# Attention's score maxima: 192 of 1024 pieces copied to SBUF by ScalarE and joined three at a time by VectorE

## The reference

```python
h = _layernorm(x) * (1 + ca) + sa
qkv = einsum('bsi,oi->bso', h, w_qkv) + b_qkv          # 16 heads of 16
attn = einsum('bhqd,bhkd->bhqk', q, k) * scale
attn = softmax(attn, axis=-1)                          # over 1024 keys
vals = einsum('bhqk,bhkd->bhqd', attn, v)
x = x + ga * (vals @ w_o.T + b_o)
# then: layernorm, a gate over 32 experts (top 6), experts, a shared expert
```

## Time and profile before

| What | Value |
|---|---|
| three runs | 1542.15, 1539.56, 1530.76 us (median 1539.56) |
| span of the profiled execution | 1412.3 us |
| TensorE busy | 1342.8 us (95%) |
| VectorE busy | 1134.9 us (80%) |
| ScalarE busy | 753.7 us (53%) |
| GpSimd busy | 606.9 us (43%) |

### The profile page before, as it was taken

The page is one execution under the profiler, slowest core; times in us unless marked ns, Lnnn a source line. Parts: engine busy times, 40 slices in busy tenths (PEclk is TensorE's granted clock), DMA queues, the critical chain, the costliest instruction groups (busy, mean ns, idle before and its releaser), DMA issues.

```text
span 1412.3 us, 30839 instructions
## 1 busy us (share of the span) xinstructions
PE 1342.8 (95%) x8191; PEld 672.8 (48%) x8192; DVE 1134.9 (80%) x2823; ACT 753.7 (53%) x1155; POOL 606.9 (43%) x782
## 2 busy tenths in 40 slices
PE   7997999999999999999999999999999999999895
PEld 4552222332333323323333232568788888888551
DVE  7886999999999999999999994566566656656588
ACT  3762477676767676777677768113343433334100
POOL 4000113143644534636346357527755555655300
PEclk9997799999999999999999999999999999999999
DMA  6898355533546345444464355947766665666698
GB/s 218 260 270 216 93 171 133 121 85 83 125 126 156 91 121 149 132 96 107 125 170 117 105 155 176 274 136 234 231 199 206 202 183 177 180 179 178 238 344 337
DMA packets 216958, 243.55 MB, mean 172 GB/s; under 512 B 93948, under 2 KB 181500, under 8 KB 216736
## 3 DMA queue, kind: packets, MB, share of 16 engines
q1 hardware_dynamic: 189328, 166.42, 43.6%
q0 software_dynamic: 21776, 68.07, 13.4%
q10 hardware_dynamic: 5760, 7.87, 1.7%
HBM read 133.98 MB, written 108.28 MB: 172 GB/s over the span
## 4 chain that ended last, share of the span: by engine, by line
PE 71%; DVE 13%; DMA 4%; issue 1%; SPq 1%; ACT 1%; POOL 0%; DVEq 0%; POOLq 0%
PE psO L1174 14%; PE ex_psGU L1682 13%; PE psE L1161 13%; PE psM L1151 9%; DVE piece_max L1048 9%; PE ex_psY L1697 7%; PE ex_psX L1671 3%; PE psM L505 2%; PE ex_psA L1691 2%; PE psGU L1495 1%; DMA wide<-results 1%; PE co_psS L1951 1%; PE late_psGU L1931 1%; PE late_psX L1942 1%; PE psM L524 1%
## 5 line engine op out<-in xcount | busy, mean ns | idle before, releaser
L1048 DVE TENSOR_REDUCE piece_max<-psM 128x1 f32<-128x512 f32 x1024 | 641.9, 680 | 27.3 <-PE psM L1151 24.0
L1115 ACT ACTIVATE wide<-psE 128x1024 f32<-128x1024 f32 x512 | 496.8, 1021 | 206.2 <-PE psE L1161 204.1
L1151 PE MATMUL psM<-wide 48*128 48x512 bf16 x1024 | 324.0, 395 | 19.9 <-DVE piece_max L1048 11.7
L1161 PE MATMUL psE<-wide 49*128 49x512 bf16 (+1 forms) x2048 | 328.7, 380 | 3.2 <-DMA wide<-maxima 2.8
L1763 POOL DMA_INDIRECT results<-vals_inv,places x223 | 213.9, 959 | 150.5 <-DVE vals_inv L1749 86.4
L1174 PE MATMUL psO<-wide 128*32 128x512 f32 x2048 | 273.6, 606 | 0.6 <-ACT wide L1115 0.6
L1151 PEld LDWEIGHTS psM<-wide 48*128 48x128 bf16 x1024 | 78.1, 93 | 348.1 <-DVE piece_max L1048 277.3
L1682 PE MATMUL ex_psGU<-wide,ex_xT 128*128 x892 | 231.3, 382 | 0.8 <-ACT ex_xT L1714 0.7
L1161 PEld LDWEIGHTS psE<-wide 49*128 49x128 bf16 (+1 forms) x2048 | 117.6, 95 | 92.3 <-issue 8.7
L1682 PEld LDWEIGHTS ex_psGU<-wide,ex_xT 128*128 128x128 f32 x892 | 152.1, 190 | 14.6 <-issue 2.3
L1714 ACT ACTIVATE ex_xT<-ex_psX 128x256 f32<-128x256 f32 x223 | 85.3, 383 | 121.3 <-PE ex_psX L1671 118.5
(11 more groups left out here) (281 smaller groups left out, 1262.8 us busy)
## 6 DMA issues: line engine op xcount, KB each, us to landing
wide<-qk_parts SPq DMA_DIRECT2D x384, 64.0 KB
wide<-results SPq DMA_DIRECT2D x16, 1536.0 KB, 9.5
rows<-lists SPq DMA_DIRECT2D x112, 160.0 KB
h2Ts<-lists SPq DMA_DIRECT2D x111, 160.0 KB
qk_parts<-parts SPq DMA_DIRECT2D x32, 384.0 KB, 3.1
xin<-in_x_dram SPq DMA_DIRECT2D x16, 512.0 KB, 4.2
v_values<-vst SPq DMA_DIRECT2D x32, 256.0 KB, 3.5
wide<-v_values SPq DMA_DIRECT2D x16, 512.0 KB
```

The lines of the kernel that those rows point to most:

```text
L1048: v.tensor_reduce(piece_max[:, qh, (x * PAIRS + h) * KT // QH + qt, kh:kh + 1], bank_of("piece", PIECES * group + n), AX.X, ALU.max, negat ...
L1115: nc.scalar.activation(probs[:, step % 2, 2 * pair:2 * pair + 2], psE[:, pair], ACT.Exp, scale=HD ** -0.5).then_inc(exp_ok, 1)
L1151: nc.tensor.matmul(bank_of(*user), qa[g][rows, h, qt * P:(qt + 1) * P], ka[g][rows, h, kh * 512:(kh + 1) * 512], start=True, stop=True).th ...
L1161: mm = nc.tensor.matmul(psE[:, pair, x], k[g][part, pair, kt * P:(kt + 1) * P], q[g][part, pair, qh * 512:(qh + 1) * 512], start=(q is qa) ...
```

## The change

ScalarE copies the third of the four pieces of a step to SBUF as bf16 in six of the eight steps of a half (p = 0, 1, 2 and 4, 5, 6), behind its exponentials, its hosted work and the copy of `psO`. These 192 pieces are not reduced by VectorE one by one. Three copies, lying side by side in one of two buffers (taken from `act_s` and from the last part of `x2`, which are not in use in attention), make a triple. VectorE joins a triple with three pairwise maxima that halve the width (512 to 256, 128, 64 for each of the three) and one negated reduction of 3x64. The first triple is joined in the step with p = 4, the second in that with p = 7: level 0 behind the first piece, levels 1 and 2 behind the second, the reduction behind the third. `finish` waits for the join too. The banks of the copied pieces are free once ScalarE's copy is done (`piece_held`), those of the others by `piece_read`, whose counts are adapted.

```diff
--- before.py
+++ after.py
@@ -734,6 +734,9 @@
     HALF_PIECES = PIECES // QH
     COLS = HG * KT // QH
     PAIRS = HG // 2
+    STEPS_HALF = HALF_PIECES // 4
+    HELD_PIECE, HELD_STEPS, TRIPLE = 2, (0, 1, 2, 4, 5, 6), 3
+    JOINED_IN = {4: 0, 7: 1}
     NGR = B * NG
     ALL = STEPS * NGR
     with ExitStack() as ctx:
@@ -747,14 +750,17 @@
         inverse = sb("inverse", [HG * HD, S // HD], F32)
         spare_to = env.h2Ts[:, 0].rearrange("p k t -> p (k t)").bitcast(I32).rearrange("p (e f) -> p e f", e=E)
         piece_max = sb("piece_max", [P, QH, COLS, 2], F32)
+        held = [of.bitcast(BF16)[:, 0:TRIPLE * 512].rearrange("p (n k) -> p n k", n=TRIPLE)
+                for of in (env.act_s[:].rearrange("p m t -> p (m t)"),
+                           env.x2[:, TPC * LAST:].rearrange("p i d -> p (i d)"))]
         neg_max = sb("neg_max", [P, HG * KT], BF16)
         neg_max_t = sb("neg_max_t", [P, HG * KT], BF16)
         psE = ctx.enter_context(nc.psum_tensor("psE", [P, 2, 2, 512], F32))
         psM = ctx.enter_context(nc.psum_tensor("psM", [P, RING, 512], F32))
         psO = ctx.enter_context(nc.psum_tensor("psO", [P, 512], F32))
-        (scored, exp_ok, summed, piece_done, piece_read, max_ready, max_stored, max_there, o_read,
+        (scored, exp_ok, summed, piece_done, piece_read, piece_held, joined, max_ready, max_stored, max_there, o_read,
          o_stored, den_stored, den_in, divided, inv_stored, ch) = (
-            env.sem("att_" + n) for n in ("scored", "exp_ok", "summed", "piece_done", "piece_read",
+            env.sem("att_" + n) for n in ("scored", "exp_ok", "summed", "piece_done", "piece_read", "piece_held", "joined",
                                           "max_ready", "max_stored", "max_there", "o_read", "o_stored", "den_stored", "den_in", "divided", "inv_stored", "chain"))
         env.inv_stored = inv_stored
         env.exp_ok, env.summed, env.piece_read, env.o_read, env.o_stored = exp_ok, summed, piece_read, o_read, o_stored
@@ -779,11 +785,26 @@
             c, w = divmod(step, WINDOW)
             return c - 1, w
 
+        def held_at(n):
+
+            return n % 4 == HELD_PIECE and n // 4 % STEPS_HALF in HELD_STEPS
+
+        def held_before(n):
+
+            halves, n = divmod(n, HALF_PIECES)
+            return len(HELD_STEPS) * halves + sum(held_at(m) for m in range(n))
+
+        def read_before(n):
+
+            return n - held_before(n)
+
         ring = Ring(HALF_PIECES, PIECES * NGR)
 
         def bank_of(*user):
 
             return psM[:, ring.bank[user]] if user in ring.bank else None
+
+        env.pieces_read = read_before(PIECES * NGR)
 
         def pieces_for(step):
 
@@ -1048,10 +1069,35 @@
                 v.tensor_reduce(piece_max[:, qh, (x * PAIRS + h) * KT // QH + qt, kh:kh + 1], bank_of("piece", PIECES * group + n),
                                 AX.X, ALU.max, negate=True).then_inc(piece_read, 1)
 
+            def join(half, triple, level):
+                of = held[triple]
+                if level < 3:
+                    width = 256 >> level
+                    if level == 0:
+                        dve.wait_ge(piece_held, TRIPLE * (2 * half + triple + 1))
+                    else:
+                        chain.ready()
+                    chain.then(v.tensor_tensor(of[:, :, 0:width], of[:, :, 0:width], of[:, :, width:2 * width], ALU.max))
+                else:
+                    chain.ready()
+                    at = HELD_STEPS[TRIPLE * triple]
+                    v.tensor_reduce(piece_max[:, half % QH, at:at + TRIPLE, HELD_PIECE // 2], of[:, :, 0:64], AX.X, ALU.max,
+                                    negate=True).then_inc(joined, 1)
+
+            def piece_or_join(group, n):
+                if not held_at(n):
+                    piece_maximum(group, n)
+                p, r = n // 4 % STEPS_HALF, n % 4
+                if p in JOINED_IN:
+                    half, triple = QH * group + n // HALF_PIECES, JOINED_IN[p]
+                    for level in ((0,), (1, 2), (3,), ())[r]:
+                        join(half, triple, level)
+
             def finish(k):
                 part = piece_max[:, k % QH]
                 cols = slice(COLS * (k % QH), COLS * (k % QH + 1))
-                dve.wait_ge(piece_read, HALF_PIECES * (k + 1))
+                dve.wait_ge(piece_read, read_before(HALF_PIECES * (k + 1)))
+                dve.wait_ge(joined, 2 * (k + 1))
                 chain.link(v.tensor_tensor(neg_max[:, cols], part[:, :, 0], part[:, :, 1], ALU.min))
                 wait(dve, max_stored, 4 * 16 * k)
                 v.transpose(neg_max_t[:], neg_max[:]).then_inc(max_ready, 1)
@@ -1073,7 +1119,7 @@
 
             v.memset(neg_max[:], 0.0).then_inc(env.zeroed, 1)
             for n in range(HALF_PIECES):
-                piece_maximum(0, n)
+                piece_or_join(0, n)
             dve.wait_ge(env.zeroed, 1)
             finish(0)
             for fixed in (env.gmax[:, :, GROUPS:], env.masked[:, :, E:], env.gkeys[:], env.keys[:]):
@@ -1085,7 +1131,7 @@
                 for n in range(4):
                     beside(step, n)
                     if group < NGR:
-                        piece_maximum(group, first + n)
+                        piece_or_join(group, first + n)
                 if group < NGR and (first + 4) % HALF_PIECES == 0:
                     finish(QH * group + first // HALF_PIECES)
             env.divide_last = lambda: divide(NGR - 1)
@@ -1107,6 +1153,18 @@
                 if c >= 0 and pair == 1 and w == GATE:
                     half_scores(act, env, c, bank_of(c, w))
 
+            def hold(group, n):
+                at = held_before(PIECES * group + n)
+                triple, slot = divmod(at, TRIPLE)
+                act.wait_ge(piece_done, PIECES * group + n + 1)
+                if slot == 0:
+                    wait(act, joined, triple - 1)
+                nc.scalar.activation(held[triple % 2][:, slot], bank_of("piece", PIECES * group + n), ACT.Copy
+                                     ).then_inc(piece_held, 1)
+
+            for n in range(HALF_PIECES + 4 * AHEAD):
+                if held_at(n):
+                    hold(0, n)
             for step in range(ALL):
                 for pair in range(2):
                     act.wait_ge(scored, 2 * step + pair + 1)
@@ -1120,6 +1178,10 @@
                     copy_out(group, 0)
                 if s == 0 and group:
                     copy_out(group - 1, 1)
+                to, first = pieces_for(step)
+                for n in range(first, first + 4):
+                    if to < NGR and held_at(n):
+                        hold(to, n)
             copy_out(NGR - 1, 1)
 
         @block.tensor
@@ -1130,8 +1192,10 @@
                 if before is None:
                     return
                 c, w = before
-                if c == "piece":
-                    pe.wait_ge(piece_read, w + 1)
+                if c == "piece" and held_at(w % PIECES):
+                    pe.wait_ge(piece_held, held_before(w + 1))
+                elif c == "piece":
+                    pe.wait_ge(piece_read, read_before(w + 1))
                 elif w in (PROJECT, PROJECT + 1):
                     pe.wait_ge(env.x2_ok, 2 * c + w - PROJECT + 1)
                 elif w in (TURN, TURN + 1):
@@ -1518,7 +1582,7 @@
             shared_in(0, 0, 0)
             rest_in(0)
             shared_in(1, 0, 0)
-            pe.wait_ge(env.piece_read, 2 * HG * KT * B * NG)
+            pe.wait_ge(env.piece_read, env.pieces_read)
             pe.wait_ge(env.placed_read, LAST)
             shared_out(0)
             rest_in(1)
```

## The result

The changed kernel takes 1627.26 us (median of four runs, 1624.02 to 1633.76), the kernel before beside it 1540.74 (1530.76 to 1542.15): ratio 1.058, 95% interval 1.052 to 1.064, 86.5 us slower. The forecast of 1562 had the sign and not the size; 1627 lies beyond its range.

The account below looks back on a forecast made before the run. TensorE and VectorE were taken to bind together, with three banks between them. Terms 11.3 - 0.7 + 0 + 12.7 - 0.8 gave +22.5 us on a span of 1412.3, plus 127 outside it: 1562 us, range 1537 to 1602.

Parts of the forecast that it names:

- Plain halves: Halves without other work: late joins outweigh the gain in plain steps, +0.63 us each, +11.3 us over 18 halves.
- The join with `finish`: Join in step 4 of 8, with `finish` behind it: the step loses 0.80 us more, with or without the reciprocal.
- The join in step 1: Join in the step after the first of a half: next first piece 0.2 us late, net +0.13.
- Copy and ScalarE: ScalarE's copies in held steps: 0.60 us each, ScalarE full but not over, busy 115 us more in attention.
- rival D: ScalarE is full in some 140 held steps: 12 us on top, 1574 us; chance 0.12.
- A: Rival: VectorE's total over a half decides, not single pieces, so the change is faster: 1517 us; chance 0.07.
- B: Rival: the joins' maxima run at the fp32 rate: 1605 us; chance 0.13.
- Prologue: Before the first score: 32 pieces become 26 and two joins on VectorE, -0.8 us.
- Turn and gate: Steps 21, 22 and 23 of a chunk: the copy queues behind ScalarE's hosted work, TensorE waits; +12.7 us over 6 chunks.
- rival C: The copy's delay behind hosted work is hidden, and half the plain loss goes too: 1545 us; chance 0.22.
- the halves with projections: 7 halves hosting projections: the join mostly fits while TensorE projects and VectorE waits; -0.1 us each, -0.7 in all.
- Routing tail: 6 halves where VectorE is the bound: five held pieces less, 3.0 us, against joins of 2.8; taken as 0.

Follow-up runs that it names:

- a0: The changed kernel, unedited, run again at the faster level: 1516.77 us, ratio 1.070, +98.7 us against the kernel before.
- b0: The kernel before, unedited, profiled a second time: 1419.26 us, ratio 1.001.
- e1: The changed kernel with ScalarE's copy ahead of its hosted work in steps 21, 22 and 23: 1502.69 us, ratio 1.060 to the kernel before.
- e2: The changed kernel with each copy reduced by itself in the places of the join, no two-operand maxima: 1506.27 us, ratio 1.061 to the kernel before.
- e4: The changed kernel with the copy ahead of the hosted work and the copies reduced singly, no pairwise maxima: 1482.93 us, ratio 1.045 to the kernel before.
- e8: The changed kernel, copy ahead of hosted work, 15 of 64 joins (beside GpSimd's instructions) done by three single reductions: 1459.80 us, ratio 1.027 to the kernel before.
- e6: The kernel before plus only 192 tiny two-input maxima (128x4, bf16) at the places of the joins: 1468.87 us, ratio 1.036.
- e5: The changed kernel, copy ahead of hosted work, no pairwise maxima, every copy reduced alone one step later: 1439.38 us, ratio 1.014 to the kernel before.

## Why the prediction was wrong

The direction was right, and two of its reasons were (the bursts at the end of a half, the copy behind the hosted work). But they make up some 31 of the 98.7 us, so that the sign came out right is in part luck: the largest single term, 44.4 us, is one that the forecast put at nothing.

**Plain halves: right in kind, a third too small.** The eight steps from 15 take 21.61 in after and 20.62 in the profile of before, the eight from 23 take 21.12 and 20.23: +0.9 to +1.0, forecast +0.63, over 18 halves 17 us instead of 11.3. Held steps run at 2.40 to 2.41, as forecast. The join with `finish` costs 0.62 over two steps (2.96 and 2.97 for 2.49 and 2.82; with the reciprocal 2.96 and 3.37 for 2.49 and 3.22), forecast 0.80. The join in step 1 costs 0.51 (2.70 and 2.79), forecast 0.13. One such end of a half in the timeline of after:

```profile
164.61 1.07 PE L1238 MATMUL psO<-wide 128*32 128x512 f32 x8
164.88 0.55 DVE L1080 TENSOR_TENSOR x<-x 128x768 bf16<-128x768 bf16 x1
...
165.95 0.64 DVE L1080 TENSOR_TENSOR x<-x 128x384 bf16<-128x384 bf16 x2
...
167.11 0.34 DVE L1084 TENSOR_REDUCE piece_max<-x 128x3 f32<-128x192 bf16 x1
...
167.57 1.06 PE L1238 MATMUL psO<-wide 128*32 128x512 f32 x8
```

Against the earlier trace rows the weighted values come 2.96 apart, not 2.48. The loss is already there in the join's own step, and the next one, with the reciprocal, doesn't hold 4.0, as I had written, but 3.37.

**Copy and ScalarE: right.** 597 ns each, 114.5 us in all, forecast 115. ScalarE's busy time in attention rose by 97.2 (519.1 to 616.3, the windows of a0), because nine of the copies (5.4 us) come before this stretch and because busy time counts the overlap with the instructions on either side once: 12 us, 0.07 a copy. So "ScalarE busy 115 us more" was not quite met, though the copies last as forecast. ScalarE does not bound the plain step; rival D is false, and so are A (no step below 2.40) and B (no maximum at 0.96).

**Prologue: right.** The first weighted values start at 156.91 in a0 and 157.66 in b0, 157.02 in after and 157.48 in before: -0.75 and -0.46, forecast -0.8.

**Turn and gate: right.** 13.6 by e1, forecast 12.7; rival C is false. The order interacts with the rest: 23.8 between e2 and e4.

**The joins beside GpSimd: here the forecast failed.** For the halves with projections the step "a late `finish` costs 0.4, lighter pieces give back as much; -0.1 each, -0.7" held that the join fits while TensorE projects. It counted TensorE's 2 us as time in which VectorE is free, and the join at w = 20 (and that of step 33) as one of a plain half, 1.50 long. It did not ask what GpSimd does then: it multiplies (w = 9) and scales and adds (w = 20) in SBUF, and a two-operand maximum from SBUF stands still meanwhile. In place of next to nothing stand 44.4 us (e8): about 4.1 a chunk at w = 9 to 11, where the forecast had -0.1, and 1.7 at w = 19 to 23. The Trainium skill says it: "SBUF — State Buffer", section "Who interferes with whom", has a VectorE instruction with two SBUF inputs contend with a GpSimd instruction that reads SBUF, where one with a single input, outside the modes that use both ports, doesn't. The traces agree on VectorE's side (2.67 us for a maximum of 0.15 in e6; none of the reductions of e2 and e8 held). On GpSimd's side they differ from the page: its `TENSOR_SCALAR` reads SBUF as well, and 21 maxima beside it in e6 were not held. I had looked up the rate of the maxima, and not what they share.

The trace of before had a sign of it, far from attention: at 11.08 us a VectorE instruction over 128x4 elements (L110, median 0.17) lasts 1.62, and at 14.78 one over 128x256 (L286, median 0.41) lasts 1.74, both while GpSimd's MEMSETs run. These are operations of another kind and the hold is only read from the overlap, but it was a reason to ask what the two engines share.

**What a stall costs.** All sums took a wait of TensorE at its length. Of the 96 us, 44 are matmuls that run slower behind the stalls, shown by the windows of a0 and b0. So a microsecond of waiting cost about 1.9 (96 / 52, an average over all of attention).

**Routing tail: small miss.** Forecast 0, measured +1.2 a chunk in a0 at w = 24 to 31. e2 to e4, with longer joins, have +2.7 to +3.2 there: VectorE's sum counts, as the forecast said.

**Sums of the forecast.** Rival A counts a join as 1.45 and the routing halves and the prologue as 1.40, where the forecast's own join is 1.50. With 1.50 rival A is 1520 and not 1517; nothing else of weight changes.

**The base.** 1412.3 + 22.5 + 127: by the ratio the forecast was +1.5%, measured +5.8 and +7.0%. Adding the 127 was harmless only by luck, because the runs of after fell at the same level as the three times shown.

**What stays open.** In a0 44.4 us are the held joins, 13.6 the order; the remaining 40.7 are e8's, and its bursts weren't removed by themselves. By the traces some 17 of them lie in the plain halves and some 7 in the routing tail (6 x 1.2); the rest is not assigned. e5 shows that evening out 192 reductions is worth 43.5, in a kernel with single reductions. Its own 21.4 are not settled.

## What to carry to other kernels

Before a VectorE operation with two SBUF operands is put into a stream, look at what GpSimd does in the same microseconds: beside one with two tensor operands a maximum over four elements can last as long as GpSimd's instruction, while a reduction with one operand isn't touched. Where two engines are full and three banks lie between them, when the work comes counts more than how much it is: the same 192 reductions cost 65 us in bursts of three and 21 when no step has more than one extra. And a stall of TensorE costs more than its length, so look at the granted clock behind it.

## What the runs showed of the hardware that was not expected

- A 128x4 maximum on VectorE, 151 ns in the median, lasted 2675 ns beside a GpSimd product of 2.37 us (e6). 192 of them cost 3.6% of the program, and only 15 of them were held.
- Of GpSimd's instructions, `TENSOR_TENSOR` (two tensors) held such maxima; in e6 `TENSOR_SCALAR` (one tensor, 1.22 us) and `DMA_INDIRECT` (0.96 us) didn't.
- Behind a wait of 2.53 us in after TensorE was granted 1.2 GHz for nearly all of the next 6.4 us (0.51), and 0.76 on average over 14 us from the beginning of the stall; in e2 it was granted 0.62 over 13 us behind four waits of 0.20 to 0.92 within 5 us, though it was busy for nearly all of these 13. The weighted values took 1.93 instead of 1.06.
- The same kernel took 1418 or 1527 to about 1540 us, with the difference mostly behind attention. In the changed kernel the chain that ended last has 8% in SyncE's queue and 9% in issue at the slower level (after), 1% and 2% at the faster one (a0). The runs near 1418 were on chips 12, 1 and 2, those near 1527 on chip 5, and the chip of the first runs isn't recorded; so it may go with the chip, and what makes it was not found.
